# The factor of the coupling update made whole by ScalarE behind the tanh, in place of a part that VectorE adds ahead of it

## What is computed

```
gf  = sigmoid(mlp3(mean over the tokens of x))          # one number per sequence
out = x
repeat 3 times:
    tf       = sigmoid(mlp4(out))                       # one number per token
    coupling = 0.1 + adaptive_range * (0.7*gf + 0.3*tf - 0.5) * 2
    out      = out + coupling * twist(out)              # twist: [o_r,o_i,p_r,p_i] -> [p_r,-p_i,-o_r,o_i]
```

## Time and profile before

| | |
|---|---|
| Device time, median of 3 runs | 3965.78 us (3965.1 to 3969.94) |
| The profiled execution | 3967.66 us, its span 3965.6 us |
| TensorE busy | 3602.5 us (91%) |
| VectorE busy | 2502.5 us (63%) |
| ScalarE busy | 1835.8 us (46%) |
| GpSimd busy | 956.9 us (24%) |
| Granted TensorE clock, mean | 0.94 |

### The profile page before, as it was taken

One profiled execution on the slowest core, in us unless ns is written; L12 is line 12 of the kernel. 1 busy time (PEld: TensorE's weight loads), 2 busy tenths in 40 slices (PEclk: granted clock), 3 DMA queues, 4 the chain that ended last, 5 costly groups with the idle time before them and its releaser, 6 DMA issues.

```text
span 3965.6 us, 57876 instructions
## 1 busy us (share of the span) xinstructions
PE 3602.5 (91%) x21952; PEld 2088.8 (53%) x21952; DVE 2502.5 (63%) x5003; ACT 1835.8 (46%) x2885; POOL 956.9 (24%) x1030
## 2 busy tenths in 40 slices
PE   2678999999999999999999999999999999999866
PEld 1344546555555555556555555555555555555433
DVE  2446566776757676675767668576766757676442
ACT  1133454545455454545445454545545454554422
POOL 0212232231313223131222313122231313222111
PEclk9788999999999999999999999999999999999867
DMA  3000000000000000000000000000000000000000
GB/s 84 1 1 1 1 1 12 1 12 1 1 12 1 11 1 12 1 1 12 1 12 1 12 1 6 6 1 12 1 12 1 6 6 1 12 1 6 1 6 6
DMA packets 39662, 27.26 MB, mean 7 GB/s; under 512 B 18464, under 2 KB 38496, under 8 KB 39392
## 3 DMA queue, kind: packets, MB, share of 16 engines
q1 hardware_dynamic: 39392, 23.56, 2.0%
HBM read 15.17 MB, written 8.39 MB: 6 GB/s over the span
## 4 chain that ended last, share of the span: by engine, by line
PE 86%; ACT 7%; DVE 4%; issue 1%; POOL 1%; DMA 0%; ACTq 0%; DVEq 0%; POOLq 0%
PE ps L494 78%; PE ps L505 8%; ACT PR L1142 2%; ACT other L1168 2%; ACT L1142 2%; DVE MX L923 1%; DVE G L961 1%; DVE MX L917 1%; ACT L1070 0%; DVE XN L834 0%; ACT other L1072 0%; DVE stats L825 0%; POOL rstd L1213 0%; PE ps L586 0%; ACT other L1080 0%
## 5 line engine op out<-in xcount | busy, mean ns | idle before, releaser
L1142 ACT ACTIVATE PR<-ps 128x1024 f32<-128x1024 f32 (+4 forms) x720 | 538.5, 795 | 635.4 <-PE ps L494 633.3
L494 PE MATMUL ps<-MAT 32*128 32x512 f32 (+5 forms) x4928 | 597.1, 492 | 47.2 <-ACT PR L1142 39.2
L923 DVE TENSOR_REDUCE MX<-ps 128x2 f32<-128x1024 f32 (+3 forms) x512 | 392.6, 820 | 280.3 <-PE ps L494 277.9
L494 PEld LDWEIGHTS ps<-MAT 32*128 32x128 f32 (+2 forms) x4928 | 282.6, 185 | 333.7 <-issue 203.9
L1213 POOL TENSOR_TENSOR rstd<-var,neg_half 128x4 f32<-128x4 f32 x144 | 148.5, 1031 | 1247.0 <-DVE var L817 1068.4
L494 PE MATMUL ps<-XT,cn_w 128*128 128x256 f32 x1536 | 386.3, 408 | 4.8 <-DVE XT L861 4.8
L1271 POOL TENSOR_SCALAR_AFFINE_SELECT PR<-PR 128x512 f32<-128x512 f32 x256 | 171.7, 671 | 787.0 <-ACT PR L1142 717.5
L494 PE MATMUL ps<-other,cn_w 128*128 128x512 f32 (+2 forms) x1152 | 334.5, 491 | 19.9 <-ACT other L1072 6.7
L494 PEld LDWEIGHTS ps<-XT,cn_w 128*128 128x128 f32 x1536 | 305.8, 204 | 87.4 <-issue 36.9
L917 DVE TENSOR_REDUCE MX<-ps 128x2 f32<-128x1024 f32 (+6 forms) x256 | 220.3, 903 | 185.7 <-PE ps L494 185.4
L494 PE MATMUL ps<-HI 32*128 32x256 f32 (+4 forms) x3072 | 219.8, 375 | 110.7 <-ACT PR L1142 75.7
(11 more groups left out here) (157 smaller groups left out, 5969.9 us busy)
## 6 DMA issues: line engine op xcount, KB each, us to landing
X<-in_L_attn_x SPq DMA_DIRECT2D x16, 512.0 KB, 3.9
out<-X SPq DMA_DIRECT2D x16, 512.0 KB, 2.9
w_up<-in_L_attn_W SPq DMA_DIRECT2D x1, 1024.0 KB, 7.1
w_down<-in_L_attn_W SPq DMA_DIRECT2D x1, 1024.0 KB, 8.9
w_krope<-in_L_attn_W_krope SPq DMA_DIRECT2D x1, 512.0 KB, 4.0
w_qk<-in_L_attn_Wqkv SPq DMA_DIRECT2D x4, 128.0 KB, 4.2
cn_w<-in_L_ffn_cn_w SPq DMA_DIRECT2D x1, 256.0 KB, 2.8
w_qrope<-in_L_attn_W_qrope SPq DMA_DIRECT2D x1, 256.0 KB, 2.9
```

The costliest lines, as they stand in the source:

```text
L494: return pe.matmul(dst, lhsT, rhs, start=start, stop=stop, skip_group_check=True)
L923: last = dve.tensor_reduce(MX[:, t, at], src[:, :, a:a + nk[pair]], AX_X, ALU.max)
L1142: freed(act.activation(PR[0:m, tile_of((s, q, g, kt)), 2 * pair:2 * pair + 2, q0:T], ps[0:m, b:b + 2, 0:T - q0], ACT.Exp, scale=SCALE[s]), ...
```

## The change

The column `gc_h[:, c, 3:4]` is made by ScalarE right behind its tanh (an Identity with scale and bias from columns). Behind the two tanh of a cycle ScalarE runs two more Identity instructions over 256 tokens each, in place, from SBUF, with scale `c_tf` and bias `gc_h[:, c, 3:4]`, so that `TF` holds the whole factor c. VectorE's `context_and_twist` and the buffer `ZT` are gone; `mixed` waits for ScalarE's new signal and does four plain two-input instructions per half: two products, an add and a subtract. The order of the steps is kept.

```diff
@@ signals
         second_moved = Signal("second_moved", cycles)
+        coupling_ready = Signal("coupling_ready", cycles)
+        context_ready = Signal("context_ready", [st[1:3] for st in steps_of("h3") if st[3] == 0])
@@ VectorE
-                def context_and_twist(s, q, k):
-                    c, a = q % CH, area_of[s]
-                    if k == 0:
-                        read_out(dve, "gc", s, q, 2)
-                        link(dve.tensor_scalar(gc_h[:, c, 3:4], gc_h[:, c, 2:3], c_gf, c_base, ALU.mult, ALU.add))
-                        for f in range(KT):
-                            read_out(dve, "xt", s, q, f)
-                    else:
-                        for ready in (first_moved, second_moved):
-                            dve.wait_ge(ready.sem, ready.at(s, q, k - 1, 1))
-                    dve.scalar_tensor_tensor(ZT[:, a, 0, :], XT[:, c, 1, :], gc_h[:, c, 3:4], XT[:, c, 0, :],
-                                             ALU.mult, ALU.add)
-                    link(dve.scalar_tensor_tensor(ZT[:, a, 1, :], XT[:, c, 0, :], gc_h[:, c, 3:4], XT[:, c, 1, :],
-                                                  ALU.mult, ALU.subtract))
-
                 def mixed(s, q, k):
                     c, a = q % CH, area_of[s]
                     for v in range(2):
-                        read_out(dve, "tf", s, q, k, v)
+                        dve.wait_ge(coupling_ready.sem, coupling_ready.at(s, q, k, v))
                         tok = slice(v * T // 2, (v + 1) * T // 2)
-                        dve.scalar_tensor_tensor(WT[:, a, tok], TF[:, a, tok], c_tf, XT[:, c, 0, tok], ALU.mult, ALU.mult)
-                        link(dve.scalar_tensor_tensor(TF[:, a, tok], TF[:, a, tok], c_tf, XT[:, c, 1, tok],
-                                                      ALU.mult, ALU.mult))
-                        dve.tensor_tensor(XT[:, c, 0, tok], ZT[:, a, 0, tok], TF[:, a, tok],
+                        dve.tensor_tensor(WT[:, a, tok], TF[:, a, tok], XT[:, c, 1, tok], ALU.mult)
+                        link(dve.tensor_tensor(TF[:, a, tok], TF[:, a, tok], XT[:, c, 0, tok], ALU.mult))
+                        dve.tensor_tensor(XT[:, c, 0, tok], XT[:, c, 0, tok], WT[:, a, tok],
                                           ALU.add).then_inc(first_moved.sem, 1)
-                        dve.scalar_tensor_tensor(XT[:, c, 1, tok], ZT[:, a, 1, tok], -1.0, WT[:, a, tok],
-                                                 ALU.mult, ALU.subtract).then_inc(second_moved.sem, 1)
+                        dve.tensor_tensor(XT[:, c, 1, tok], XT[:, c, 1, tok], TF[:, a, tok],
+                                          ALU.subtract).then_inc(second_moved.sem, 1)
@@ ScalarE, third_layer, k == 0
                               "gc", s, q, 2)
+                        read_out(act, "gc", s, q, 2)
+                        act.activation(gc_h[:, q % CH, 3:4], gc_h[:, q % CH, 2:3], ACT.Identity, scale=c_gf,
+                                       bias=c_base).then_inc(context_ready.sem, 1)
@@ ScalarE, fourth_layer, behind the two tanh
+                    if k == 0:
+                        act.wait_ge(context_ready.sem, context_ready.at(s, q))
+                    for v in range(2):
+                        read_out(act, "tf", s, q, k, v)
+                        own = TF[:, area_of[s], v * T // 2:(v + 1) * T // 2]
+                        act.activation(own, own, ACT.Identity, scale=c_tf,
+                                       bias=gc_h[:, q % CH, 3:4]).then_inc(coupling_ready.sem, 1)
```

More of the change, by code:

```diff
@@ L197, in build @@
         H2, H3, TF, WT = (other[:, :, a:a + 512] for a in (1024, 1536, 2048, 2560))
-        ZT = other[:, :, 3072:4096].rearrange("p a (m n) -> p a m n", m=2)
         U = other[:, :, :].rearrange("p a (j n) -> p a j n", j=8)
@@ L1011, in _ @@
                         normalize(*a)
-                    elif name == "h3":
-                        context_and_twist(*a)
                     elif name == "tf":
```

## The result

The changed kernel takes 4006.1 us (median of four runs, 4004.75 to 4006.52) against 3965.4 us for the kernel before on the same chip (3956.93 to 3969.94): ratio 1.0105, 95% interval 1.0087 to 1.0122. It is 1% slower, some 41 us, where 7.3 us were forecast. The time lies above the range. What happened is the rival named "the clock catches more turns", to which I had given 0.14, and in more turns than I had priced there. The profiled execution took 4004.75 us, with a span of 4003.0 us, 37.4 us longer than before.

What follows compares the result with a forecast made beforehand. TensorE was taken to bound the kernel (busy 91% of the span). Start and end 3.2, tf.A.0 2.0 and tf.C.1 2.1 made 7.3 us: 3975.0 us from the profiled execution, 3973.1 from the median; range 3957 to 3991.

Steps and rivals of the forecast that it cites:

- the clock catches more turns: Rival, slower: five more of the thirteen middle turns become long, 17.5 us on top, 3990 us; chance 0.14.
- the 13 middle turns keep their clock: Assumption of the sum: the middle turns, 2983.8 us in all, change only by the small delays added to them.
- tf.A.0: Cycle in stage A: TensorE's h1.A.1 comes to wait for XT, 0.14 us in 14 sequences, 2.0 us (bounds 0 and 8.5).
- tf.C.1: Cycle in stage C where `mixed` collides with GpSimd: 0.15 us later in 14 sequences, 2.1 us (bounds -1.4 and +5.6).
- Start and end: Waits in sequences 0, 1 and the last: 1.8 + 0.6 + 0.9 + 0.6 - 0.7 = 3.2 us.
- L929: Last sequence: TensorE waited 0.73 us for this instruction, which stood behind removed L850; 0.7 us taken off.
- `back`: Last sequence: it waits for the second half of L861, which comes later; +0.6 us.
- Busy times: VectorE falls by about 173 us, ScalarE rises by 90 to 120; the Identity takes near 0.57 us (bounds 0.48 and 0.78).
- the 19 places of the forecast: Some 19 places where the Identity's length counts: its bounds shift the sum by -1.7 or +4.0 us; SBUF rule about 2 higher.
- The table: Rival: Identity behind tanh needs a switch of ScalarE's function table, 25 us on TensorE's path, 3991 us; chance 0.03.
- The sign: Chances for the whole kernel: faster 0.15, same within 0.2% 0.43, slower 0.42.

Runs made afterwards that it cites:

- e9: The change in cycle tf.A.0 alone, the other five cycles of a turn as in the kernel before: 3990.8 us, ratio 1.0069.
- e14: The kernel before with one extra VectorE product over 448 elements ahead of the update of tf.A.0, making XT late: 3974.5 us, ratio 1.0018.
- e3: The changed kernel with ScalarE's order tanh, Identity, tanh, Identity in place of tanh, tanh, Identity, Identity: 3988.7 us, ratio 1.0060.
- e6: The change in the three cycles of stage C alone, stage A as in the kernel before: 3960.1 us, ratio 0.9980.
- e7: The change in all cycles except tf.A.0, which is as in the kernel before: 3965.2 us, ratio 0.9988.
- e4: The changed kernel with TensorE doing h2.C.0 ahead of exp.E.1.1, filling its wait for exponents: 3967.7 us, ratio 1.0006, no long turn.
- e13: The kernel before with only the TensorE order of e4 (h2.C.0 ahead of exp.E.1.1): 3960.4 us, ratio 0.9980.
- e2: The kernel before with two unread Identity instructions on ScalarE behind each pair of tanh: 3967.7 us, ratio 1.0003.
- e15: The kernel before with two extra VectorE products (448 and 320 elements) ahead of the update of tf.A.0: 3997.8 us, ratio 1.0079.
- e5: The change in the three cycles of stage A alone, stage C as in the kernel before: 3975.7 us, ratio 1.0020.
- e10: The changed kernel with TensorE doing content.E.1 ahead of h1.A.1, to cover the wait for XT: 3988.0 us, ratio 1.0066.
- e11: The change in stage C alone, with the TensorE order of e4: 3961.3 us, ratio 0.9998.
- e1: The kernel before with one more, overwritten TensorE product of 128 columns in tf.A.0: 3971.7 us, ratio 1.0014.
- e8: The kernel before with one more, overwritten TensorE product of 256 columns in tf.A.0: 3966.8 us, ratio 0.9994.

## Why the prediction was wrong

- **The step that failed** is that the 13 middle turns keep their clock: the sum added its delays to turns of unchanged length, and a change in the number of long turns was a rival at 0.14, priced at five more. There were eight more, and three turns of 229.4 gone besides. "Against: only three were longer than 231" was a poor argument. It counted what the clock had done and did not ask how near the short turns were to the long form. TensorE's busy time, +30.2 us for the same instructions, is the whole error: in each long turn two stretches ran at 1.2 GHz and took 3.4 us more than in a short one.
- **tf.A.0** was sized right and judged wrongly. The wait is 0.15 us where 0.14 was forecast, and 2.0 us were booked for it. By e9 the cycle alone costs 27 us, though its own waits are 1.2 us in the middle: the loss lies 44 us later in the turn. By e14 a late XT is enough to bring a little of that about, and by e3 much of the loss comes without a wait for XT.
- **tf.C.1**: 0.11 us later against 0.15 forecast, by the mechanism that I had read (VectorE's product comes out 0.29 us behind GpSimd's). The working of the forecast gave 0.34 - 0.15 = 0.19, of which 0.15 was taken without a reason. But it costs the kernel nothing: e6 and e7, which have it, are not slower. TensorE's idle time in the 13 turns grew by 1.3 us, where tf.A.0 and tf.C.1 together were to give 4 in 14.
- **Start and end**: 3.2 us forecast, 11.1 measured. The start's waits are as I had them, mostly. Sequence 0 waits 2.66, 2.66 and 4.5 us for XT in place of 2.01, 2.06 and 4.0: +0.6 each. Sequence 1 waits 1.73 in place of 0.72 (+1.0, forecast +0.6) and for the attention output 1.9 in place of 0.9 (+1.0, forecast +0.9). That makes 3.8 where I had 3.3. Of the rest of the 7.2 us, 1.3 is busy time, and most of what remains is a wait for `LT` in sequence 1 that I had not looked for: 1.69 us, where the kernel before has none. TensorE came to it earlier: the two products ahead of it ran at full clock (2.00 and 1.94 us in place of 3.68 and 3.73). At the end both terms came as forecast (no wait for L929, `back` waits 0.60 us), TensorE's idle time is unchanged, and the 3.9 us are all busy time of the same instructions, so the clock's.
- **Waiting in all**: TensorE's idle time grew by 7.2 us, and the sum was 7.3. That the totals agree is partly luck: 1.3 and not 4 in the middle, 5.9 and not 3.2 at start and end, of which 1.7 is the wait for `LT` that an earlier TensorE brought.
- **Busy times**: VectorE fell by 196 us (forecast 173; the products also got shorter, 563 and 636 ns to 500 and 534) and ScalarE rose by 95 (forecast 90 to 120). The Identity took 0.60 us against 0.57. The Trainium skill (VectorE: DVE Perf Modes, section on the TRN2 errata) has a ScalarE read of SBUF 0.04 us dearer than one of PSUM; the estimate by that rule, 0.61, is nearer to the 603 ns measured. No run here separates this from other causes. At the 19 places of the forecast, 0.04 to 0.08 us later are 0.8 to 1.5 us, less than the 2 that were set down for it.
- **The table**: no additional load, as argued.
- **The sign** was missed through this too: slower by over 0.2% had 0.42, beside 0.43 for no change.

Shown: that the loss is half clock (the rows above) and can be taken back with the change kept (e4, beside e13), that tf.A.0 is needed for it (e7) and brings two thirds of it alone (e9), and that two Identity instructions on ScalarE do not (e2). A late XT by itself is enough for a small part (e14, 0.2%); e15 lost 0.8%, by turns of another form. Open: why a change at h1.A.1 decides on stretches 44 us later; why e5, with more of the change, loses less than e9; why e9 has more long turns than e14; how e3 has long turns without a wait for XT; and whether another delay of TensorE at that place would do the same. e10, which took the wait away, brought others and settles nothing on that.

One thing the timelines show and I had overlooked: the wait for XT stands right ahead of multiplications that are partly at half clock in every middle turn of both kernels (the granted clock was 0.85 from 918.2 to 928.0 us in the kernel after). The sixteen of h1.A.1 take 5.11 us in a turn of the kernel before and 5.14 in one of the kernel after, and 3.62 in e10, where content.E.1 stands ahead of them. That a shift there moves where later stretches fall is likely, and not shown.

## What to carry to other kernels

When turns of equal work come in two lengths, find the stretch that differs and the wait ahead of it before forecasting; a change whose own delays are a tenth of a microsecond moved nearly all turns to the other length here. Compare TensorE's busy time for the same count of instructions: it grew here by 30 us, which was the clock, and the list of waits did not show it. When an experiment adds work to test a delay, look whether the next wait swallowed it. The remedy need not be at the place of the change: here moving one step away from behind a wait of 1.2 us gave back what the change had cost.

## What the runs showed of the hardware

The turns settle. In the kernel after, eleven turns in a row took 232.08 to 232.13 us, the last seven of them 232.11; in e4 the last seven took 228.69. In e11, which has neither the wait at h1.A.1 nor the change around it, most are again 228.68 or 228.69: what it saves in a turn does not show in the turn's length. The multiplications of h1.A.1, in a turn of e4 and in one of e11:

```profile
2751.60 5.14 PE L495 MATMUL ps<-XT,cn_w 128*128 128x256 f32 x16
```

```profile
2745.92 5.28 PE L500 MATMUL ps<-XT,cn_w 128*128 128x256 f32 x16
```

They start 14.02 us into the turn in e4, behind a wait, and 13.77 in e11, and take 0.14 us longer where they start earlier: more of them is at half clock. So part of a saved wait comes back as busy time at once. Between the two lengths lie the same instructions and twice 1.7 us at 1.2 GHz. I had expected the granted clock to follow the load, a little more or less of it, and not to jump by 3.4 us per turn for 0.15 us of waiting, nor to jump back when a wait of the same length is moved by a few multiplications.

Holding XT back by one product of VectorE (e14, waits of up to 0.3 us) loses 0.2%, by two (e15, up to 0.7 us) 0.8%. Some 0.2 and 0.4 us of more work for TensorE ahead of its wait for exponents (e1, e8) lose 0.1% and nothing, because that wait gets shorter by as much. The four runs do not tell whether idling weighs more than work of the same length.
